# One scan instruction over two channel blocks in a selective state-space kernel

## Chip, core and metric

The kernel runs on one core of a Trainium2 chip. The metric is the device time of one execution, in microseconds (us). Before the change the median is 7764.41 us.

## What is computed

Two Mamba layers over 8192 steps and 1024 channels with 16 states each, with normalisation around them, and then a soft mixture of experts. The change is in the recurrence of the Mamba layers, which stands in the reference as:

```
dA = jnp.exp(jnp.einsum('bld,dn->bldn', delta, A))
dBu = jnp.einsum('bld,bln,bld->bldn', delta, Bm, u)
def step(h, inp):
    dA_t, dBu_t, C_t = inp
    h = dA_t * h + dBu_t
    return (h, jnp.einsum('bdn,bn->bd', h, C_t))
```

Before it come an input projection, a causal convolution of 4 taps with SiLU, the projections that give delta, B and C, and a softplus. After it come the skip u*D, the gate silu(z) and the output projection.

## The kernel before

**Tiling.** The sequence is cut into 16 chunks of T = 512 steps. Both layers give 32 chunks, numbered G. The 1024 channels are 8 blocks of 128 (the partitions). A chunk has 128 *slots*: k, b = divmod(slot, 4). Of k (0 to 31), k // 16 is the half (which 4 blocks) and k % 16 the state n; b is the block in the half. Two neighbouring slots are a *pair*, 0 to 63, and a chunk has 64.

**Per slot.** ScalarE (ACT) writes decay = exp(delta * -A) into a PSUM ring of 4 tiles (L855). GpSimd (POOL) writes bu = w * B for the two blocks of a pair in one instruction of 1024 elements (L1082) into a ring of 3 pairs. VectorE (DVE) scans a slot, h = decay * h + bu over 512 steps (L1162). The scan's first state is h_last of the chunk before, which ACT saves once per k, so 32 times per chunk (L888). TensorE (PE) then turns the four blocks of state k into PSUM, 128 steps at a time (tile ("state", k, j), L591), and acc += C * turned follows: three of four such tiles go to DVE as SCALAR_TENSOR_TENSOR (L1182), the fourth to ACT as a product (L871), which POOL sums (L1097, L1106). For even k it is tile j = 0 that goes to ACT, for odd k it is j = 3.

**The turn ring.** All turned tiles of a chunk (128 states, 8 "skip" tiles of u*D, L599, which ACT copies into acc at L878, and 8 "y" tiles, L607, which DVE gates at L1191) use two PSUM banks in turn. PE fills a bank only when the tile before the last one has been taken. A state tile of group k stands one slot after its group: tile (k, j) at slot 4k + 5 + j. ACT takes its tiles two slots after the slot where they stand. The first STT of a half into acc waits for ACT's copy of that skip tile.

**The order.** Every engine runs an order written out beforehand, slot by slot. At each slot DVE has its scan, then the turned tiles of that slot. PE has the turned tiles of the slot, then matmuls of the projections of this and the next chunk, which a timetable spreads. ACT has the decay, then products and copies, then what it takes from the projections. Four times a chunk it applies SiLU to four blocks (L760 and L798), with a table load ahead and one behind, at slots 43 and 65 (u), 116, and slot 1 of the next chunk (z). POOL has, per pair, the sums and products of delta at the pairs of W_AT, then bu, then the sums of SUM_AT.

The waits that the change touches are:

```
act.wait_ge(scanned, G * SLOTS_BODY + (s + 1 - DEC_RING + C_SCAN))        # decay_of
pool.wait_ge(scanned, G * SLOTS_BODY + (s + 2 - 2 * BU_RING + C_SCAN))    # inputs
dve.wait_ge(decay_set, G * SLOTS_BODY + (s + 1))                          # scan
dve.wait_ge(bu_set, G * PAIRS + (s // 2 + 1 + C_BU))
```

## Time and profile before

| | before |
|---|---|
| median of 3 runs | 7764.41 us (7763.73 to 7766.31) |
| span of the profiled execution | 7761.4 us |
| DVE busy | 7373.2 us, 95% |
| PE busy | 7045.9 us, 91% |
| POOL busy | 6604.5 us, 85% |
| ACT busy | 5872.5 us, 76% |

The 32 chunks fill the time from about 90 us to about 7190 us; the mixture of experts is the rest. The profiled execution is one run of its own. Instructions of an engine overlap at their ends, so what one costs in a queue is the distance of two starts, and that is less than its duration.

### The profile page before, as it was taken

How to read it: one execution, taken by the hardware profiler on the slowest of the kernel's cores; microseconds unless marked ns; L12 is line 12 of the kernel's file. 1: busy time of each engine (PE TensorE's matmuls, PEld its weight loads, DVE VectorE, ACT ScalarE, POOL GpSimd, SP SyncE). 2: the span in 40 equal slices, each digit the busy share in tenths (PEclk: the TensorE clock that was granted, in tenths of full speed). 3: DMA queues.
4: the chain of work that ended last, by engine and by line, in shares of the span. 5: the costliest groups of instructions: out<-in, count | busy, mean ns of one | idle time of the engine just before them, and what ended most of it. 6: DMA issues, size and time to landing. Idle time of an engine off the chain costs nothing. (4 is left out here: it accounts for less than half of the span.)

```text
span 7761.4 us, 100822 instructions
## 1 busy us (share of the span) xinstructions
PE 7045.9 (91%) x31116; PEld 4002.2 (52%) x31116; DVE 7373.2 (95%) x8275; ACT 5872.5 (76%) x11175; POOL 6604.5 (85%) x2871
## 2 busy tenths in 40 slices
PE   7899999999999999999999999999999999987799
PEld 3555555555555555554555555545555555554664
DVE  6999999999999999999999999999999999999655
ACT  7787788887877888777777777777777777775564
POOL 5999999999999999999999999999999999998010
PEclk9999999999999999999999999999999999998899
DMA  2221121112221211122211111111111111111665
GB/s 91 60 66 66 61 66 59 55 62 66 66 66 61 66 59 55 62 68 66 66 50 56 48 52 54 55 55 56 49 55 50 51 54 55 55 50 41 246 232 184
DMA packets 230984, 549.66 MB, mean 71 GB/s; under 512 B 27120, under 2 KB 27376, under 8 KB 210864
## 3 DMA queue, kind: packets, MB, share of 16 engines
q1 hardware_dynamic: 201776, 491.81, 19.9%
q10 hardware_dynamic: 28672, 51.39, 1.8%
q8 instruction: 252, 4.13, 0.2%
q14 instruction: 284, 2.33, 0.1%
HBM read 441.39 MB, written 101.71 MB: 70 GB/s over the span
## 5 line engine op out<-in xcount | busy, mean ns | idle before, releaser
L1082 POOL TENSOR_TENSOR bu<-w,b_rep 128x1024 f32<-128x1024 f32 x2048 | 4806.9, 2365 | 541.8 <-DVE h L1162 532.5
L1162 DVE TENSOR_TENSOR_SCAN h<-decay,h_last,bu 128x512 f32<-128x512 f32 x3840 | 4813.9, 1274 | 13.9 <-ACT decay L855 13.9
L591 PEld LDWEIGHTS turn<-ident_m,h 128*128 128x128 f32 x16384 | 1952.1, 142 | 2702.7 <-DVE acc L1182 1315.3
L855 ACT ACTIVATE decay<-delta,neg_a 128x512 f32<-128x512 f32 x4096 | 2777.4, 690 | 647.6 <-DVE h L1162 609.5
L591 PE MATMUL turn<-ident_m,h 128*128 128x128 f32 x16384 | 2558.2, 280 | 421.0 <-DVE acc L1182 348.2
L1182 DVE SCALAR_TENSOR_TENSOR acc<-turn,c_now,acc 128x512 f32<-128x512 f32 x3072 | 2243.7, 730 | 72.1 <-ACT c_now L883 43.1
L871 ACT ACTIVATE prod<-turn,c_now 128x512 f32<-128x512 f32 x1024 | 701.0, 685 | 504.2 <-PE turn L591 369.0
L1097 POOL TENSOR_TENSOR prod<-prod 128x1024 f32<-128x1024 f32 x448 | 1057.6, 2361 | 10.6 <-ACT prod L871 10.6
L513 PE MATMUL proj<-x_conv,w_in 128*128 128x512 f32 x2048 | 1046.3, 603 | 4.5 <-ACT x_conv L845 1.3
L513 PE MATMUL proj<-x_gate,w_in 128*128 128x512 f32 x2048 | 1019.8, 595 | 0.0
L513 PE MATMUL proj<-conv_in,conv_diag 128*128 128x512 f32 x1984 | 996.6, 594 | 0.0
L513 PE MATMUL proj<-zy,w_out 128*128 128x512 f32 x1024 | 505.6, 596 | 23.0 <-ACT u L756 20.5
L513 PE MATMUL proj<-w_out,zy 128*128 128x512 f32 x1024 | 504.4, 599 | 0.9 <-DVE zy L1191 0.9
L513 PEld LDWEIGHTS proj<-x_conv,w_in 128*128 128x128 f32 x2048 | 328.3, 193 | 123.5 <-issue 91.7
L513 PEld LDWEIGHTS proj<-x_gate,w_in 128*128 128x128 f32 x2048 | 324.1, 191 | 98.0 <-issue 91.8
L1162 DVE TENSOR_TENSOR_SCAN h<-decay,zeros_m,bu 128x512 f32<-128x512 f32 x256 | 320.1, 1272 | 46.7 <-POOL bu L1082 43.6
L513 PEld LDWEIGHTS proj<-conv_in,conv_diag 128*128 128x128 f32 x1984 | 313.8, 191 | 90.7 <-issue 89.1
L1064 POOL TENSOR_TENSOR delta<-delta,w 128x1024 f32<-128x1024 f32 x128 | 302.4, 2362 | 40.7 <-ACT w L789 40.7
L599 PE MATMUL turn<-d_diag,u 128*128 128x128 f32 x2048 | 288.6, 285 | 48.5 <-DVE acc L1182 44.2
L738 ACT ACTIVATE conv_diag<-ident_m,par 128x128 f32<-128x128 f32 x992 | 316.5, 394 | 0.4
L1071 POOL TENSOR_TENSOR w<-delta,u 128x1024 f32<-128x1024 f32 x128 | 302.5, 2363 | 0.3
L599 PEld LDWEIGHTS turn<-d_diag,u 128*128 128x128 f32 x2048 | 252.9, 194 | 74.3 <-DVE acc L1182 60.1
(161 smaller groups left out, 5690.6 us busy)
## 6 DMA issues: line engine op xcount, KB each, us to landing
b_rep<-b_rows SPq DMA_DIRECT2D x1024, 256.0 KB, 3.3
x_gate<-xt SPq DMA_DIRECT2D x32, 1024.0 KB, 7.0
xt<-stage ACTq DMA_DIRECT2D x128, 256.0 KB, 2.4
x_conv<-xt SPq DMA_DIRECT2D x31, 1024.0 KB, 6.9
x_gate<-in_x_dram SPq DMA_DIRECT2D x16, 1024.0 KB, 6.7
x_l<-in_x_dram SPq DMA_DIRECT2D x16, 1024.0 KB, 9.5
m_l<-xt SPq DMA_DIRECT2D x16, 1024.0 KB, 7.8
x<-x_l SPq DMA_DIRECT2D x16, 1024.0 KB, 6.3
```

What stands on the lines that cost most here:

```text
L513: mm = pe.matmul(out[0:lhs.shape[1], :], lhs, rhs, start=n == 0, stop=n == count - 1)
L591: mm = pe.transpose(out[:, b * P:(b + 1) * P], h[:, (G * GROUPS + k) % H_RING, b, j * P:(j + 1) * P], ident[:])
L599: mm = pe.matmul(out[:, b * P:(b + 1) * P], u[:, hf * HB + b, j * P:(j + 1) * P], d_diag[:, hf * HB + b, :], start=True, stop=True)
L738: act.activation(conv_diag[:, b % 2, k, :], ident[:], ACT.Copy, scale=par[:, STATES + k, b:b + 1])
L855: act.activation(decay[:, (G * SLOTS_BODY + s) % DEC_RING, :], delta[:, blk, :], ACT.Exp, scale=neg_a[:, n, blk:blk + 1]).then_inc(decay_s ...
L871: act.activation(prod[:, V_BUFFER[q], k % 2, :], turn[:, BANK[tile], :], ACT.Copy, scale=c_now[:, j, n:n + 1]).then_inc(v_done, 1)
L1064: pool.tensor_tensor(delta[:, lo:lo + 2, :], delta[:, lo:lo + 2, :], w[:, lo:lo + 2, :], ALU.add).then_inc(delta_set, 1)
L1071: pool.tensor_tensor(w[:, lo:lo + 2, :], delta[:, lo:lo + 2, :], u[:, lo:lo + 2, :], ALU.mult).then_inc(w_set, 2)
L1082: pool.tensor_tensor(bu[:, (G * PAIRS + s // 2) % BU_RING, :, :], w[:, blk:blk + 2, :], b_rep[:, g % B_RING, :].unsqueeze(1).to_broadcast( ...
L1097: pool.tensor_tensor(total, total, prod[:, V_BUFFER[q]], ALU.add).then_inc(vsum_set, 1)
L1162: dve.tensor_tensor_scan(h[:, (G * GROUPS + k) % H_RING, b, :], decay[:, (G * SLOTS_BODY + s) % DEC_RING, :], bu[:, (G * PAIRS + s // 2) % ...
L1182: dve.scalar_tensor_tensor(out, src, scalar, out, ALU.mult, ALU.add).then_inc(x_done, 1)
```

## The change

The scan now runs once per pair, over 1024 elements. The two blocks stand one behind the other, so at element 0 of each the decay is set to zero once at the start (DVE writes column 0 of the decay ring; ACT writes columns 1 to 511 only), and bu's column 0 holds the block's first state instead of the product (POOL writes columns 1 to 511). With a zero decay the state there becomes exactly that value. The first states of a half chunk (16 states x 4 blocks) are worked out ahead: POOL multiplies A and delta at step 0 ("exponent"), ACT takes the exponential, POOL forms w * B at step 0, multiplies the exponential by h_last and adds ("state"). ACT copies two columns per pair into bu (head). B at step 0 goes through DRAM: ACT stores 16 values, SP loads them to all partitions. Three entries of W_AT move to earlier pairs. DVE's order within a pair becomes: scan, then all turned tiles of both slots. ACT's becomes: head, both decays, then everything else of both slots.

```diff
-W_AT = {13: ('sum', 2), 19: ('product', 2), 25: ('sum', 3), 27: ('product', 3), 47: ('sum_next', 0), 51:
-        ('product_next', 0), 56: ('sum_next', 1), 63: ('product_next', 1)}
+W_AT = {13: ('sum', 2), 19: ('product', 2), 25: ('sum', 3), 27: ('product', 3), 47: ('sum_next', 0), 50:
+        ('product_next', 0), 53: ('sum_next', 1), 57: ('product_next', 1)}
+HEAD_AT = {26: ('exponent', 1), 30: ('state', 1), 54: ('exponent_next', 0), 62: ('state_next', 0)}
+HEAD_EXP_AT = {57: ('exp', 1), 115: ('exp_next', 0)}
+BFIRST_AT = 24
...
+        def load_first(X):
+            sp.wait_ge(bfirst_stored, X * 16 + 16)
+            if X > 0:
+                sp.wait_ge(hfirst_set, 2 * X)
+            sp.dma_start(b_first[:], d["b_row_first"][X].partition_broadcast(P)).then_inc(bfirst_in, 16)
...
+                if k == BFIRST_AT and not kind.last:
+                    load_first(G + 1)
...
-            act.activation(decay[:, (G * SLOTS_BODY + s) % DEC_RING, :], delta[:, blk, :], ACT.Exp,
+            act.activation(decay[:, (G * SLOTS_BODY + s) % DEC_RING, 1:T], delta[:, blk, 1:T], ACT.Exp,
...
+        def head(G, p):
+            k, pr = divmod(p, 2)
+            hf, n = divmod(k, STATES)
+            if p % (PAIRS // 2) == 0:
+                act.wait_ge(hfirst_set, 2 * G + hf + 1)
+            act.wait_ge(scanned, G * SLOTS_BODY + (2 * (p - BU_RING) + 2 + C_SCAN))
+            act.copy(bu[:, (G * PAIRS + p) % BU_RING, :, 0], h_first[:, hf, n, 2 * pr:2 * pr + 2]).then_inc(head_set, 1)
...
-                    decay_of(G, kind, k, b)
+                    if b % 2 == 0:
+                        head(G, s // 2)
+                        decay_of(G, kind, k, b)
+                        decay_of(G, kind, k, b + 1)
...
-            pool.tensor_tensor(bu[:, (G * PAIRS + s // 2) % BU_RING, :, :], w[:, blk:blk + 2, :],
-                               b_rep[:, g % B_RING, :].unsqueeze(1).to_broadcast([P, 2, T]), ALU.mult).then_inc(bu_set, 1)
+            pool.tensor_tensor(bu[:, (G * PAIRS + s // 2) % BU_RING, :, 1:T], w[:, blk:blk + 2, 1:T],
+                               b_rep[:, g % B_RING, 1:T].unsqueeze(1).to_broadcast([P, 2, T - 1]), ALU.mult).then_inc(bu_set, 1)
+        def first_exponent(X, hf):
...
+            pool.tensor_tensor(a_first[:], neg_a[:, :, blks], delta[:, blks, 0].unsqueeze(1).to_broadcast([P, STATES, HB]),
+                               ALU.mult).then_inc(exponent_set, 1)
+        def first_state(X, hf):
...
+            pool.tensor_tensor(h_first[:, hf], w[:, blks, 0].unsqueeze(1).to_broadcast([P, STATES, HB]),
+                               b_first[:].unsqueeze(2).to_broadcast([P, STATES, HB]), ALU.mult).then_inc(hfirst_set if fresh else first_step, 1)
...
+        dve.memset(decay[:, :, 0:1], 0.0).then_inc(heads_zero, 1)
+        def scan(G, kind, p):
+            k, pr = divmod(p, 2)
+            dve.wait_ge(decay_set, G * SLOTS_BODY + (2 * p + 2))
+            dve.wait_ge(bu_set, G * PAIRS + (p + 1 + C_BU))
+            dve.wait_ge(head_set, G * PAIRS + (p + 1))
...
+            dve.tensor_tensor_scan(h[:, (G * GROUPS + k) % H_RING, 2 * pr:2 * pr + 2, :].rearrange("p b t -> p (b t)"),
+                                   decay[:, at:at + 2, :].rearrange("p b t -> p (b t)"),
+                                   bu[:, (G * PAIRS + p) % BU_RING, :, :].rearrange("p b t -> p (b t)"), 0.0,
+                                   ALU.mult, ALU.add).then_inc(scanned, 2)
...
-                scan(G, kind, k, j)
+                if s % 2 == 0:
+                    scan(G, kind, s // 2)
```

**What moves on DVE.** First the order of DVE around slots 34 to 39 of a chunk. The rows that write h are scans, those that write acc take turned tiles. Before:

```order
L1162 SCALAR_TENSOR_TENSOR h<-decay,h_last,bu 128x512
L1182 SCALAR_TENSOR_TENSOR acc<-turn,c_now,acc 128x512
L1162 SCALAR_TENSOR_TENSOR h<-decay,h_last,bu 128x512 x3
L1182 SCALAR_TENSOR_TENSOR acc<-turn,c_now,acc 128x512
L1162 SCALAR_TENSOR_TENSOR h<-decay,h_last,bu 128x512
```

After, in the same place:

```order
L1255 SCALAR_TENSOR_TENSOR h<-decay,bu 128x1024
L1277 SCALAR_TENSOR_TENSOR acc<-turn,c_now,acc 128x512 x2
L1255 SCALAR_TENSOR_TENSOR h<-decay,bu 128x1024 x2
L1277 SCALAR_TENSOR_TENSOR acc<-turn,c_now,acc 128x512 x2
L1255 SCALAR_TENSOR_TENSOR h<-decay,bu 128x1024
```

Two takings that had a scan between them now stand next to each other. Where a gated y tile falls into a pair, three stand in a row. After, at slots 118 and 119:

```order
L1255 SCALAR_TENSOR_TENSOR h<-decay,bu 128x1024
L1277 SCALAR_TENSOR_TENSOR acc<-turn,c_now,acc 128x512
L1286 TENSOR_TENSOR zy<-turn,zy 128x512
L1277 SCALAR_TENSOR_TENSOR acc<-turn,c_now,acc 128x512
```

Before, a scan stood between the second and the third of these.

**What moves on ACT.** Now ACT's order from slot 8 to slot 10 of a chunk; the rows that write acc are copies of skip tiles. Before:

```order
L888 COPY h_last<-h 128x4
L855 ACTIVATE decay<-delta,neg_a 128x512
L878 COPY acc<-turn 128x512
L738 ACTIVATE conv_diag<-ident_m,par 128x128 x4
L855 ACTIVATE decay<-delta,neg_a 128x512
L878 COPY acc<-turn 128x512
```

After:

```order
L935 COPY h_last<-h 128x4
L925 COPY acc<-turn 128x512
L767 ACTIVATE conv_diag<-ident_m,par 128x128 x4
L898 COPY bu<-h_first 128x2
L888 ACTIVATE decay<-delta,neg_a 128x511 x2
L925 COPY acc<-turn 128x512
```

Between the two copies one decay and the head are added.

## Rows read from the trace of the kernel before

**Rows 1.** The page, busy time of each engine over the span.

```profile
PE 7045.9 (91%) x31116; PEld 4002.2 (52%) x31116; DVE 7373.2 (95%) x8275; ACT 5872.5 (76%) x11175; POOL 6604.5 (85%) x2871
```

**Rows 2.** One 500 us stretch inside the chunks: busy time by engine, clock, DMA.

```profile
3000.00:3500.00 500.00, 461.92 (x2066) 260.28 (x2065) 494.38 (x527) 394.55 (x751) 461.47 (x200) 0.99 0.19 61
```

**Rows 3.** Groups, 2000 to 6000 us: busy, mean ns | idle before, releasers.

```profile
L1162 DVE TENSOR_TENSOR_SCAN h<-decay,h_last,bu 128x512 f32<-128x512 f32 x2186 | 2740.4, 1274 | 8.2 <-ACT decay L855 8.2
L1082 POOL TENSOR_TENSOR bu<-w,b_rep 128x1024 f32<-128x1024 f32 x1158 | 2717.4, 2364 | 302.8 <-DVE h L1162 297.0 <-DMA b_rep<-b_rows 5.0
L855 ACT ACTIVATE decay<-delta,neg_a 128x512 f32<-128x512 f32 x2314 | 1568.5, 690 | 359.8 <-DVE h L1162 342.1 <-ACT stage L804 7.3 <-ACT conv_in L845 5.9
...
L1182 DVE SCALAR_TENSOR_TENSOR acc<-turn,c_now,acc 128x512 f32<-128x512 f32 x1734 | 1266.5, 730 | 37.4 <-ACT c_now L883 25.2 <-PE turn L591 12.0
...
L888 ACT COPY h_last<-h 128x4 f32<-128x4 f32 x578 | 108.4, 188 | 0.0
```

**Rows 4.** All waits of DVE, 2000 to 6000 us: total us, times, longest.

```profile
DVE acc L1182 <- ACT c_now L883: 25.2, 18, 1.4
DVE acc L1182 <- PE turn L591: 12.0, 23, 2.0
DVE h L1162 <- ACT decay L855: 10.5, 19, 1.9
```

**Rows 5.** Timeline of DVE, slots 4 to 8: start, length, instruction [idle before].

```profile
3423.87 3.64 DVE L1162 TENSOR_TENSOR_SCAN h<-decay,h_last,bu 128x512 f32<-128x512 f32 x3
3427.95 0.75 DVE L1182 SCALAR_TENSOR_TENSOR acc<-turn,c_now,acc 128x512 f32<-128x512 f32 x1 [0.44 <-PE turn L591]
3428.62 1.27 DVE L1162 TENSOR_TENSOR_SCAN h<-decay,h_last,bu 128x512 f32<-128x512 f32 x1
3429.81 0.73 DVE L1182 SCALAR_TENSOR_TENSOR acc<-turn,c_now,acc 128x512 f32<-128x512 f32 x1
3430.45 1.27 DVE L1162 TENSOR_TENSOR_SCAN h<-decay,h_last,bu 128x512 f32<-128x512 f32 x1
3433.13 0.75 DVE L1182 SCALAR_TENSOR_TENSOR acc<-turn,c_now,acc 128x512 f32<-128x512 f32 x1 [1.40 <-ACT c_now L883]
```

**Rows 6.** Timeline of ACT in the same place.

```profile
3430.14 0.59 ACT L878 COPY acc<-turn 128x512 f32<-128x512 f32 x1 [0.85 <-PE turn L599]
3430.63 1.28 ACT L738 ACTIVATE conv_diag<-ident_m,par 128x128 f32<-128x128 f32 x4
3431.81 0.68 ACT L855 ACTIVATE decay<-delta,neg_a 128x512 f32<-128x512 f32 x1
3432.42 0.58 ACT L878 COPY acc<-turn 128x512 f32<-128x512 f32 x1
```

**Rows 7.** Timeline of PE: a skip tile, and a turn that waited for DVE.

```profile
3429.05 1.06 PE L599 MATMUL turn<-d_diag,u 128*128 128x128 f32 x8
...
3433.94 0.66 PE L591 MATMUL turn<-ident_m,h 128*128 128x128 f32 x4 [0.93 <-DVE acc L1182]
```

**Rows 8.** Groups of DVE behind the chunks: one operation at two widths.

```profile
L1418 DVE TENSOR_TENSOR run_top<-run_top,logits 128x1024 f32<-128x1024 f32 x16 | 19.2, 1199 | 10.7 <-ACT logits L1454 10.7
...
L1637 DVE TENSOR_TENSOR top_d<-run_top 128x512 f32<-128x512 f32 x1 | 0.7, 693 | 0.3 <-PEq L1961 0.3
```

**Rows 9.** Timeline of ACT around one SiLU, at slot 65.

```profile
3526.11 1.28 ACT L760 ACT_TABLE_LOAD   x1
3527.40 1.91 ACT L760 ACTIVATE u<-u 128x2048 f32<-128x2048 f32 x1
3529.33 1.28 ACT L703 ACT_TABLE_LOAD   x1
3530.63 1.91 ACT L855 ACTIVATE decay<-delta,neg_a 128x512 f32<-128x512 f32 x3
```

**Rows 10.** Timeline of POOL: three bu back to back.

```profile
3408.52 6.98 POOL L1082 TENSOR_TENSOR bu<-w,b_rep 128x1024 f32<-128x1024 f32 x3
```

**Rows 11.** A small POOL operation, 2000 to 6000 us.

```profile
L1055 POOL TENSOR_TENSOR nmr_x<-neg_mean,rstd_x 128x4 f32<-128x4 f32 x5 | 1.0, 206 | 0.0
```

65 lines of the change are left out of this document (55 added, 10 removed).

## The prediction

> **What bounds the kernel now.** I read the page first: DVE is busy for 95% of the span, PE for 91%, POOL for 85% [rows 1]. Then one stretch inside the chunks: DVE 494 of 500 us, PE 462, POOL 461, ACT 395 [rows 2]. So DVE is the bound, with three engines close behind. Last I read who keeps DVE waiting. From 2000 to 6000 us there are 578 saves of h_last at 32 per chunk [rows 3], so 18.06 chunks, 221.5 us each. All waits of DVE there are 25.2 + 12.0 + 10.5 = 47.7 us [rows 4], which is 2.6 us per chunk. The other 218.9 us are DVE's instructions one behind the other. The 18 waits of 1.4 us, one per chunk, all have one place: the taking at slot 8, which needs ACT's copy of a skip tile.
>
> **What the change takes away.** One scan of two. A scan lasts 1.274 us, but costs a queue the distance of two starts: three in a row take 3.64 us, so (3.64 - 1.27) / 2 = 1.18 [rows 5]. What is its fixed part? An STT of the same width lasts 0.730, a scan 0.544 more [rows 3]. A TENSOR_TENSOR of 1024 elements lasts 1.199 against 0.693 for 512: 0.506 for 512 elements [rows 8]. I take 0.535 for a pass over 512 elements, between these two, and two passes for a scan, 1.07. What is left of 1.18 is 0.11 us, and 0.115 with 1.19 for a scan that an STT follows (3428.62 to 3429.81 [rows 5]). A pair's scan then costs 2.25 us in the queue instead of 2.37. Per chunk that is 64 x 0.115 = 7.4 us, or 236 us for 32 chunks. The bounds are nothing (a pair's scan costs two scans) and 2 x 0.693 - 1.199 = 0.19 us per pair [rows 8], 12 us per chunk.
>
> The Trainium skill, "VectorE: DVE Perf Modes", section on the TRN2 errata, says that the fixed latency is paid once per instruction, so that one large tile pays once what many small tiles pay each, and gives (N + 151) / 0.96 ns for an fp32 tensor_tensor. Its fixed 157 ns would make the gain 2048 x 0.157 = 322 us, by that page an estimate. The rows here agree on the duration (0.693 for 512) but show that neighbours overlap, so I keep 0.115.
>
> **What it adds, and what hides it.**
> - ACT: 64 head copies per chunk. A copy of 4 columns lasts 0.188 [rows 3]. ACT goes from 0.79 of a chunk [rows 2] to at most 0.84 with 64 x 0.188 = 12 us, so on average it is covered; ends of instructions overlap, and I take 0.08 each. If not covered, see below.
> - POOL: 8 small operations per chunk, each at least 0.2 [rows 11]; I take 0.3, so 2.4 us. POOL has 64 + 24 large ones at (6.98 - 2.36) / 2 = 2.31 [rows 10], 203 us. So POOL needs about 206 us per chunk against DVE's 211.5 + stalls. Adding up POOL's operations from pair 42 to pair 57, where seven extra ones now lie, gives 46.5 us against DVE's 46 and a lead of one ring: within 0.1 to 0.5. I book 0.3 us.
> - SP and the store of B's first column: one small transfer each per chunk, issued at k = 24, while ACT's store is at slot 76 (k = 19) and the consumer at pair 62. Nothing waits. Before the first chunk it is a transfer in series, about 3 us once.
>
> **The stalls that the new order makes.** Here I disagree with the plain gain. Times below are from the DVE instruction named.
> 1. *Two takings of the same bank with no scan between.* PE refills a bank only once it is taken. An STT lasts 0.73, PE starts 0.06 after it (3433.88 to 3433.94) and takes 0.66 [rows 5, 7], and the next STT starts some 0.04 behind: 1.49 us from start to start. Where an ACT tile lies between two DVE tiles (pairs 4 and 19), DVE is ready after 0.64 and loses 0.85. Where three DVE tiles stand in a row (pairs 11, 12, 13, 59, 60, 61) it is ready after 1.26 and loses 0.23. Sum: 1.7 + 1.4 = 3.1 us per chunk. Before, a scan of 1.19 covered each.
> 2. *Slot 8, the wait of 1.4 us.* Let T be the start of the STT at slot 6. PE's skip tile starts at T + 0.79 and takes 1.06, ACT's copy ends its part at T + 2.4, the four conv_diag take 1.18, then head 0.08, two decays 1.24, the copy 0.6, and DVE goes on at T + 5.6. (Before: 3427.95 to 3433.13, 5.18, with one decay of 0.61 less and PE 0.3 later [rows 5, 6].) DVE is ready at T + 2 x 0.64 + 2.25 = T + 3.53. The wait is 2.05 instead of 1.4.
> 3. *SiLU.* From the first table load to the next decay ACT is away for 3530.63 - 3526.11 = 4.52 us [rows 9]. Before, the next decay was due three scans and four or five takings after the ring let ACT go; now both decays of a pair are due together. From the end of scan p - 2: head and decays 1.36, SiLU 4.52, head and decays 1.45, so 7.35, against 2 x 2.25 + n x 0.64 for the n takings of three pairs. At slot 1, n is 4: 7.07, so a loss of 0.3 to 0.4. At slot 65, n is 4 too, and ACT arrives late in chunks with a norm: 0.3 to 0.8, I take 0.5. At slot 43 n is 6 and the 0.85 of pair 19 comes on top: none. At slot 116: none.
> 4. ACT's own lag in the crowded first half (skip copies at pairs 17, 18, norms): 0.4.
>
> Stalls after: 3.1 + 2.05 + 0.9 + 0.4 + 0.3 = 6.8 us per chunk, 4.2 more than the 2.6 of now.
>
> **The sum.** 7.4 - 4.2 = 3.2 us per chunk, 32 chunks: 102 us, less 3 us at the start: 99 us. The profiled span is 7761.4, 3.0 below the median of the runs, so the median goes from 7764.4 to about 7665, which is 1.3% faster. PE's work per chunk does not change, and its idle time in a chunk is about 17 us [rows 2].
>
> **The rivals.**
> - *A. The gain comes through.* The stalls overlap with each other, as one gives the next its slack. For it: now only 2.6 us of 221.5 are lost, with engines as full. Against it: items 1 and 2 lie in DVE's own chain, and no slack elsewhere helps them. Time: 7764.4 - 236 + 3 = 7531. Chance 0.22. The page above would give still more.
> - *B. POOL becomes the bound (slower).* Its bu rows now have 511 elements and start one element late. No row shows such a shape. POOL has 24 x 2.31 + 2.4 = 57.8 us of other work, so it equals the present chunk of 221.5 when a bu costs (221.5 - 57.8) / 64 = 2.56 us, 11% above 2.31. From there on the kernel is slower; at 2.65 the chunk is 227.4, + 189 us: 7953. For it: POOL is full to 93% as it is, so little is enough. Against: bu and the sums, of different patterns, last the same, 2.36. Chance 0.08.
> - *C. The stalls are larger than I book,* about 10 to 11.5 us: ACT, with decays that are due in twos, falls behind all through the first half. 7764 +- 35. Chance 0.14.
> - *D. The change doesn't shorten the scan:* a scan over two PSUM banks costs 2.37. Then only the stalls are left, 4.2 x 32 = 134: 7900. Against: the two passes per element of rows 3 and 8. Chance 0.06.
>
> **How the numbers follow.** My forecast has 0.50, with its own range of 7600 to 7740 (stalls 4.5 to 9 us per chunk). The range for all takes in A and most of C: 7535 to 7790; below lies the upper bound of the fixed part, above lie B and D. A measurement of this kernel tells 0.2%, 15 us, from no change. Faster: 0.50 + 0.22 + a bit of C = 0.75. Same: 0.07, from C. Slower: B, D and the rest of C, 0.18.
>
> **What would show it.** The group of scans: 128x1024, mean 2.34 us (rival D: 2.5). The waits of DVE: "acc <- c_now" of about 2.05 once per chunk where 1.4 was; "acc <- PE turn" of 0.85 twice and of about 0.2 six times per chunk; "h <- decay" about 0.9 per chunk; "h <- bu" nearly none. bu on POOL at 2.36 (rival B: above 2.6). Head copies at 0.2. If DVE's waits sum to 2.6 per chunk, A is right; if they sum to over 10, C. I would be wrong also if the three waits of a scan cost time of their own in DVE's queue, or if PE, not asked for here, is late at the second tile of most pairs.

## The result and the profile after

The changed kernel takes 7890.7 us (median of 4 runs, 7889.7 to 7891.9) against 7764.1 before. The ratio is 1.0162, with a 95% interval from 1.0148 to 1.0177: 1.6% slower, where 1.3% faster was forecast, and 101 us above the upper end of the range.

The page of the changed kernel, busy time of each engine over its span of 7889.6 us (before: [rows 1]):

```profile
PE 7014.4 (89%) x31116; PEld 4070.2 (52%) x31116; DVE 7096.4 (90%) x6228; ACT 6063.2 (77%) x13283; POOL 6671.7 (85%) x3115
```

DVE has 277 us less to do than in [rows 1], and yet the kernel takes 127 us more. So the scans got cheaper, and the gain went into waiting. The groups from 2000 to 6000 us show the same, with the columns of [rows 3]:

```profile
L1138 POOL TENSOR_TENSOR bu<-w,b_rep 128x1022 f32<-128x1022 f32 x1136 | 2669.2, 2366 | 327.3 <-DVE h L1255 327.2
L1255 DVE TENSOR_TENSOR_SCAN h<-decay,bu 128x1024 f32<-128x1024 f32 x1136 | 2567.3, 2276 | 94.5 <-ACT decay L888 79.2 <-issue 7.8 <-POOL bu L1138 4.8
L888 ACT ACTIVATE decay<-delta,neg_a 128x511 f32<-128x511 f32 x2272 | 1479.8, 686 | 312.0 <-DVE h L1255 311.6
...
L1277 DVE SCALAR_TENSOR_TENSOR acc<-turn,c_now,acc 128x512 f32<-128x512 f32 x1703 | 1199.0, 734 | 172.9 <-PE turn L620 139.9 <-ACT c_now L930 31.1
...
L898 ACT COPY bu<-h_first 128x2 f32<-128x2 f32 x1136 | 216.1, 190 | 20.2 <-ACT stage L837 14.3 <-DVE h L1255 2.7 <-ACT conv_in L878 2.5
```

The scan lasts 2.276 us where two of 1.274 stood. The shape of 511 elements costs POOL nothing (2.366 against 2.364), and a head copy costs 0.19. What has changed is the last part of the two DVE rows, the idle time before them. All waits of DVE in the same 4000 us, against 25.2 + 12.0 + 10.5 us in [rows 4]:

```profile
DVE acc L1277 <- PE turn L620: 139.9, 230, 1.9
DVE h L1255 <- ACT decay L888: 79.2, 84, 2.5
DVE acc L1277 <- ACT c_now L930: 31.1, 18, 1.7
DVE h L1255 <- issue: 7.8, 18, 0.5
DVE h L1255 <- POOL bu L1138: 4.8, 18, 0.3
DVE h L1255 <- ACT h_last L935: 2.7, 2, 1.3
```

**Figures per chunk.** From here on I use three numbers per chunk, worked out from each trace over the chunks 9 to 26 (of 0 to 31): the *period*, the mean distance between the first scans of two chunks; the *idle* time of DVE, the sum of all gaps over 30 ns before its scans and takings; and DVE's *own work*, the difference of the two. Before they are 221.4, 2.65 and 218.8 us. After they are 225.4, 15.33 and 210.1. Own work fell by 8.7 and idle time rose by 12.7, where the forecast had 7.4 and 4.2. The difference of 4.0, times 32 chunks, is 128 us, and the runs differ by 127.

Two limits of these figures. The median less 32 periods is not the same for all kernels below: 677 to 678 us for the kernel before and the changed one, 682 to 694 us for the others. So periods and medians can disagree by up to half a us per chunk, and where a price is that small I give both. And own work is not durations alone: each wait also breaks the overlap of two neighbours on DVE, and the lost overlap is counted as own work.

By pair, the idle time of DVE is (us per chunk; pairs under 0.3 in both left out):

```
pair    before  after   before it stands, after
1        0.10   0.66    scan <- decay
3        0.53   0.35    taking <- turn
4        1.40   2.48    taking <- c_now 1.73, second taking <- turn 0.75
16        -     0.35    second taking <- turn
19        -     1.82    scan <- decay 1.07, second taking <- turn 0.75
22       0.48   1.03    scan <- decay 0.88, scan <- h_last 0.15
28        -     0.32    scan <- decay
31       0.13   0.37    taking <- turn
33        -     1.57    scan <- decay
35        -     1.10    taking <- turn
55        -     1.34    second taking <- turn
59        -     2.35    taking <- turn 1.87, scan <- issue 0.43
```

### The profile page after: what moved, and what is told of

It reads as the page before. It is cut to its first block and busy times, and to the rows that moved or that the text cites. A ratio compares the mean times of both kernels' runs of the same rounds, so it can differ in the third digit from the quotient of the medians.

```text
span 7889.6 us, 101470 instructions
## 1 busy us (share of the span) xinstructions
PE 7014.4 (89%) x31116; PEld 4070.2 (52%) x31116; DVE 7096.4 (90%) x6228; ACT 6063.2 (77%) x13283; POOL 6671.7 (85%) x3115
## 3 DMA queue, kind: packets, MB, share of 16 engines
q14 instruction: 289, 2.37, 0.1%
## 5 line engine op out<-in xcount | busy, mean ns | idle before, releaser
L1138 POOL TENSOR_TENSOR bu<-w,b_rep 128x1022 f32<-128x1022 f32 x2048 | 4810.2, 2365 | 593.1 <-DVE h L1255 593.0
L1255 DVE TENSOR_TENSOR_SCAN h<-decay,bu 128x1024 f32<-128x1024 f32 x2048 | 4628.4, 2276 | 210.5 <-ACT decay L888 138.5
L620 PEld LDWEIGHTS turn<-ident_m,h 128*128 128x128 f32 x16384 | 1997.7, 143 | 2744.9 <-issue 1409.7
L888 ACT ACTIVATE decay<-delta,neg_a 128x511 f32<-128x511 f32 x4096 | 2667.8, 686 | 566.7 <-DVE h L1255 565.3
L1277 DVE SCALAR_TENSOR_TENSOR acc<-turn,c_now,acc 128x512 f32<-128x512 f32 x3072 | 2163.9, 734 | 313.2 <-PE turn L620 255.4
L542 PE MATMUL proj<-x_gate,w_in 128*128 128x512 f32 x2048 | 1040.4, 605 | 37.6 <-ACT zy L827 37.6
L898 ACT COPY bu<-h_first 128x2 f32<-128x2 f32 x2048 | 389.7, 190 | 43.8 <-ACT stage L837 25.5
```

Of the source, the lines that this page charges most:

```text
L542: mm = pe.matmul(out[0:lhs.shape[1], :], lhs, rhs, start=n == 0, stop=n == count - 1)
L620: mm = pe.transpose(out[:, b * P:(b + 1) * P], h[:, (G * GROUPS + k) % H_RING, b, j * P:(j + 1) * P], ident[:])
L888: act.activation(decay[:, (G * SLOTS_BODY + s) % DEC_RING, 1:T], delta[:, blk, 1:T], ACT.Exp, scale=neg_a[:, n, blk:blk + 1]).then_inc(dec ...
L898: act.copy(bu[:, (G * PAIRS + p) % BU_RING, :, 0], h_first[:, hf, n, 2 * pr:2 * pr + 2]).then_inc(head_set, 1)
L1138: pool.tensor_tensor(bu[:, (G * PAIRS + s // 2) % BU_RING, :, 1:T], w[:, blk:blk + 2, 1:T], b_rep[:, g % B_RING, 1:T].unsqueeze(1).to_broa ...
L1255: dve.tensor_tensor_scan(h[:, (G * GROUPS + k) % H_RING, 2 * pr:2 * pr + 2, :].rearrange("p b t -> p (b t)"), decay[:, at:at + 2, :].rearr ...
```

## What happens at two of these places

**Pair 59, behind the SiLU of slot 116.** ACT in the changed kernel (start, length, instruction, idle before):

```profile
3904.51 0.18 ACT L935 COPY h_last<-h 128x4 f32<-128x4 f32 x1
3904.71 1.28 ACT L831 ACT_TABLE_LOAD   x1
3906.01 1.92 ACT L831 ACTIVATE zy<-zy 128x2048 f32<-128x2048 f32 x1
3907.94 1.28 ACT L732 ACT_TABLE_LOAD   x1
3909.24 0.19 ACT L898 COPY bu<-h_first 128x2 f32<-128x2 f32 x1
3909.34 1.29 ACT L888 ACTIVATE decay<-delta,neg_a 128x511 f32<-128x511 f32 x2
3910.57 0.67 ACT L918 ACTIVATE prod<-turn,c_now 128x512 f32<-128x512 f32 x1
```

PE in the same place:

```profile
3908.12 1.02 PE L542 MATMUL proj<-x_gate,w_in 128*128 128x512 f32 x2
3911.29 0.66 PE L620 MATMUL turn<-ident_m,h 128*128 128x128 f32 x4 [2.14 <-ACT prod L918]
3911.78 1.10 PE L542 MATMUL proj<-x_gate,w_in 128*128 128x512 f32 x2
3912.68 1.06 PE L620 MATMUL turn<-ident_m,h 128*128 128x128 f32 x4
3913.53 1.06 PE L636 MATMUL turn<-ident_m,acc 128*128 128x128 f32 x4
3914.39 1.83 PE L542 MATMUL proj<-x_gate,w_in 128*128 128x512 f32 x2
3916.05 0.60 PE L620 MATMUL turn<-ident_m,h 128*128 128x128 f32 x4
```

And DVE:

```profile
3910.72 2.29 DVE L1255 TENSOR_TENSOR_SCAN h<-decay,bu 128x1024 f32<-128x1024 f32 x1 [0.42 <-issue]
3913.78 0.75 DVE L1277 SCALAR_TENSOR_TENSOR acc<-turn,c_now,acc 128x512 f32<-128x512 f32 x1 [0.77 <-PE turn L620]
3914.63 0.69 DVE L1286 TENSOR_TENSOR zy<-turn,zy 128x512 f32<-128x512 f32 x1
3916.70 0.75 DVE L1277 SCALAR_TENSOR_TENSOR acc<-turn,c_now,acc 128x512 f32<-128x512 f32 x1 [1.38 <-PE turn L620]
```

ACT is away for 4.5 us. Its decays then wait for nothing, but its product stands behind head and decays, and ends at 3911.24. Until then ACT holds one of the two banks, and PE, which works in order, stands for 2.14 us with its projections behind the turn. What follows is dearer than the wait: PE's four transposes take 1.06 us instead of 0.60. The windows show why (us, then busy time of PE, PEld, DVE, ACT and POOL, granted clock, DMA share, GB/s):

```profile
3905.00:3911.00 6.00, 4.15 (x19) 2.16 (x17) 5.58 (x6) 5.96 (x7) 6.00 (x4) 1.00 0.40 87
3911.00:3913.00 2.00, 1.71 (x8) 1.15 (x9) 2.00 (x1) 1.73 (x5) 2.00 (x2) 0.90 0.93 306
3913.00:3915.00 2.00, 2.00 (x9) 1.72 (x8) 1.13 (x3) 2.00 (x6) 2.00 (x1) 0.50 1.06 451
3915.00:3917.00 2.00, 2.00 (x8) 0.93 (x7) 0.62 (x2) 0.36 (x1) 1.92 (x5) 0.75 0.81 331
```

The granted clock is 0.50 for 3.4 us, which is 1.2 instead of 2.4 GHz, beginning 1.3 us after PE's idle time. DVE has little to scan just here (it gates a y tile and takes), so both of PE's late tiles show: 0.77 and 1.38 us.

How much of this is the clock can be read from the same trace. In all 18 chunks PE stands idle here for 2.14 or 2.15 us, but in 4 of them the clock stays at 1.00. One of the four, DVE:

```profile
3235.53 0.75 DVE L1277 SCALAR_TENSOR_TENSOR acc<-turn,c_now,acc 128x512 f32<-128x512 f32 x1 [0.28 <-PE turn L620]
...
3237.27 0.75 DVE L1277 SCALAR_TENSOR_TENSOR acc<-turn,c_now,acc 128x512 f32<-128x512 f32 x1 [0.39 <-PE turn L620]
```

Without the fall DVE's takings at pair 59 wait 0.66 us in each of the four, with it 2.24 to 2.34 us in each of the 14 others. The heavy DMA traffic of the stretch shown is not the reason: in chunks 11, 17, 22 and 25, which have a fall here too, DMA's share is at most 0.12 there and the takings wait 2.27 to 2.34 us. So a fall costs DVE 1.6 us here, and PE's idle time without one 0.66. Pair 35 is alike: 0.70 us in the 13 chunks without a fall at pair 33, 2.02 to 2.23 us in the 5 with one. Together the falls at these two places make 1.7 of the 15.3 us of idle time per chunk in this one profiled execution.

**Pair 55, a moved sum on POOL.** POOL in the changed kernel, then ACT:

```profile
3889.77 4.70 POOL L1138 TENSOR_TENSOR bu<-w,b_rep 128x1022 f32<-128x1022 f32 x2
3894.39 2.38 POOL L1180 TENSOR_TENSOR prod<-prod 128x1024 f32<-128x1024 f32 x1
3896.70 2.38 POOL L1138 TENSOR_TENSOR bu<-w,b_rep 128x1022 f32<-128x1022 f32 x1
```

```profile
3893.42 0.69 ACT L918 ACTIVATE prod<-turn,c_now 128x512 f32<-128x512 f32 x1
3896.87 0.69 ACT L918 ACTIVATE prod<-turn,c_now 128x512 f32<-128x512 f32 x1 [2.76 <-PE turn L620]
```

The product of 3896.87 starts 0.1 us after POOL's sum over earlier products ends (3894.39 + 2.38 = 3896.77). The view names the turn as its releaser, but the turn it reads was done at 3895.5 (0.60 us from 3894.94), so it is the sum that frees the product's buffer. ACT then gives its bank back late, and DVE's second taking waits 1.34 us (3898.34 to 3899.68). POOL is late there, since its steps on delta stand at pairs 50, 53 and 57 instead of 51, 56 and 63, with an exponent at 54. That was a reading; the kernels *no_heads_w* and *w_late2* below test it.

## The experiments

Each was timed beside the kernel before, whose median stayed between 7763.7 and 7765.3 us. The first group walks from the kernel before to the changed one, the last splits the gain.

| kernel | median us | ratio to before (95%) | period | idle | own work |
|---|---|---|---|---|---|
| before | 7764.1 | 1 | 221.4 | 2.65 | 218.8 |
| order_act | 7819.7 | 1.0071 (1.0056 to 1.0086) | 223.1 | 4.21 | 218.9 |
| order_dve | 7900.9 | 1.0176 (1.0161 to 1.0191) | 225.5 | 5.39 | 220.1 |
| order_both | 7904.7 | 1.0181 (1.0166 to 1.0196) | 225.6 | 5.74 | 219.9 |
| pair_sync | 7969.0 | 1.0262 (1.0247 to 1.0277) | 227.6 | 7.33 | 220.2 |
| no_heads_w | 7762.1 | 0.9996 (0.9986 to 1.0006) | 220.8 | 10.88 | 209.9 |
| no_heads | 7797.6 | 1.0042 (1.0028 to 1.0056) | 222.4 | 12.34 | 210.0 |
| copies_only | 7822.8 | 1.0073 (1.0058 to 1.0088) | 222.8 | 12.71 | 210.1 |
| after | 7890.7 | 1.0162 (1.0148 to 1.0177) | 225.4 | 15.33 | 210.1 |
| w_late2 | 7835.6 | 1.0093 (1.0076 to 1.0110) | 223.6 | 13.55 | 210.0 |
| after_no_tables | 7752.0 | 0.9984 (0.9975 to 0.9994) | 220.8 | 10.92 | 209.9 |
| before_no_tables | 7748.3 | 0.9978 (0.9969 to 0.9988) | 220.8 | 2.14 | 218.7 |
| skip_early | 7911.3 | 1.0187 (1.0170 to 1.0204) | 225.6 | 15.38 | 210.2 |
| lag2 | 7939.3 | 1.0224 (1.0209 to 1.0239) | 226.5 | 16.49 | 210.0 |
| act_fine | 7992.5 | 1.0293 (1.0277 to 1.0308) | 228.1 | 17.27 | 210.8 |
| mixed | 7737.9 | 0.9965 (0.9952 to 0.9978) | 220.4 | 10.04 | 210.3 |
| mixed_w | 7700.8 | 0.9917 (0.9902 to 0.9932) | 219.1 | 8.80 | 210.3 |
| const_start | 7595.6 | 0.9783 (0.9769 to 0.9798) | 215.8 | 4.16 | 211.6 |
| twos_const | 7798.3 | 1.0044 (1.0027 to 1.0061) | 222.2 | 9.47 | 212.7 |
| single_all | 7675.4 | 0.9887 (0.9872 to 0.9901) | 218.2 | 6.41 | 211.8 |

### The coarse order alone: order_both, order_dve, order_act

The kernel before, with single scans of 512, in the order of the changed kernel on both engines, on DVE alone and on ACT alone:

```diff
 # DVE (order_both, order_dve)
-                scan(G, kind, k, j)
+                if s % 2 == 0:
+                    scan(G, kind, *divmod(s, J))
+                    scan(G, kind, *divmod(s + 1, J))
                 for tile in TURN_AT[s]:
 # ACT (order_both, order_act)
-                    decay_of(G, kind, k, b)
+                    if b % 2 == 0:
+                        decay_of(G, kind, k, b)
+                        decay_of(G, kind, k, b + 1)
```

> The kernel before, single scans of 512 and no first states worked out, but in the coarse order of the change: on DVE both scans of a pair and then the turned tiles of both slots, on ACT both decays of a pair and then the rest of both slots. Theory 1 (the coarse order makes the stalls): the 15.3 us of stalls per chunk seen after the change appear here too, without the gain of the merged scan: about 12 us per chunk more than before, 8150 us, at least 8000. Theory 2 (the stalls come from the work that was added on ACT and POOL, heads and first states): close to before, under 7850.

> The kernel before with DVE's coarse order alone: two scans, then the tiles of both slots; ACT as before. Theory 1: the waits of DVE's takings (PE turn and the copy at slot 8) rise as after the change, from 2.1 to 6 to 8 us per chunk, about 7900 to 7950 us, and scans wait little for decays. Theory 2: no change, 7764.

> The kernel before with ACT's coarse order alone: both decays of a pair first; DVE as before. Theory 1: scans wait for decays around the SiLUs, 2 to 3 us per chunk more, 7830 to 7860 us. Theory 2: no change, 7764.

The order alone costs 4.2 us per chunk, almost all of it on DVE (4.1 alone; ACT's alone 1.7; the two don't add). The waits of order_both, 2000 to 6000 us:

```profile
DVE acc L1184 <- PE turn L591: 60.1, 161, 0.8
DVE acc L1184 <- ACT c_now L883: 31.5, 18, 1.8
DVE h L1164 <- ACT decay L855: 7.1, 24, 2.0
```

By pair these stand where item 1 and item 2 of the prediction put them: 0.75 at pairs 4 and 19, 0.09 to 0.31 at pairs 11 to 13 and 59 to 61, and 1.75 for the skip tile. Missed were 0.35 at pair 5, 0.36 at 35 and 0.18 at 16. The idle time is 5.7 us, the forecast for the new order was 6.8. So this part of the argument holds. Own work rises by 1.1 besides: the durations of DVE's instructions sum to 0.9 less, but neighbours overlap by 17.9 instead of 19.9 us per chunk. The total of 7905 us lies between the two theories (at least 8000, under 7850). In order_act the scans hardly wait (0.09 us per chunk for decays), against what was expected: the 1.6 us more of idle time stand at the takings of pairs 4, 23 and 59.

### Giving and taking in twos: pair_sync

order_both, in which a scan waits for both decays of its pair and gives both ring places back at once, as a merged scan must:

```diff
-            dve.wait_ge(decay_set, G * SLOTS_BODY + (s + 1))
+            dve.wait_ge(decay_set, G * SLOTS_BODY + (s // 2 * 2 + 2))
...
-                                   ALU.mult, ALU.add).then_inc(scanned, 1)
+            if b % 2 == 1:
+                ins.then_inc(scanned, 2)
```

> The coarse order of both engines with single scans of 512, as in order_both, but each pair's first scan waits for both decays, and the ring places are given back once per pair: the waits of a merged scan without its speed. Order_both has 225.6 us per chunk, 5.7 of them stalls. Theory A (a merged scan stalls because it takes and gives back its inputs in twos): stalls rise to 9 us per chunk and more, 8000 us or more. Theory B (the faster DVE meets bursts of ACT, POOL and PE that it did not outrun before): as order_both, 7905, plus at most 20 us.

It costs 1.9 us per chunk more. The wait for decays goes from 0.39 to 1.83 us per chunk, at pairs 19 (0.21 to 0.82), 22 (to 0.50) and 33 (0.07 to 0.34), where the changed kernel has it too. With 7.3 us of idle time and 7969 us it too lies between its two theories (9 us and 8000, or 7925 at most).

### The merged scan without heads: no_heads_w and no_heads

The changed kernel without all that the first states need: POOL writes bu's 512 columns again and the second block of a pair goes on from column 0 with a decay of zero, so no state is carried from chunk to chunk. no_heads_w also has the old W_AT:

```diff
-                        head(G, s // 2)
-            dve.wait_ge(head_set, G * PAIRS + (p + 1))
-                    if s in HEAD_EXP_AT:
+                    if False:
-                if p in HEAD_AT:
+                if False:
 # no_heads_w besides
-W_AT = {13: ('sum', 2), 19: ('product', 2), 25: ('sum', 3), 27: ('product', 3), 47: ('sum_next', 0), 50:
-        ('product_next', 0), 53: ('sum_next', 1), 57: ('product_next', 1)}
+W_AT = {13: ('sum', 2), 19: ('product', 2), 25: ('sum', 3), 27: ('product', 3), 47: ('sum_next', 0), 51:
+        ('product_next', 0), 56: ('sum_next', 1), 63: ('product_next', 1)}
```

> No_heads (7798) with the products and sums of delta at their old pairs (51, 56 and 63 for 50, 53 and 57). What is left against pair_sync is then the merged scan alone. If the moved POOL work makes the waits at pairs 55 and 59 (1.1 and 1.5 us per chunk): 7720 to 7770, faster by 1 to 2.5 us per chunk. If those waits come from the SiLU and the turn ring: 7798 +- 15.

> The changed kernel without the first states: no head copies on ACT, no exponents and states on POOL, no load of B's first column, and POOL forms bu over all 512 columns, so each block starts from its own bu and not from the chunk before. Coarse order and merged scan stay. Theory 1: ACT has some 5 us per chunk less, which eases the SiLU places a little: 7830 to 7880. Theory 2: the stalls go, about 7530 to 7600.

From pair_sync to no_heads_w own work falls by 10.3 us per chunk (220.2 to 209.9), while idle time rises by 3.6: a DVE that is done earlier finds ACT and PE not ready. (2.2 us of it stand before scans under "issue", with no releaser in the profile, but at pairs 19 and 33, where the other kernels wait for decays.) What is left in the period is 6.7 us per chunk, about what order and twos had cost (4.2 + 1.9): the kernel stands where it stood before. (What the 10.3 consist of, twos_const tells below.) The moved sums alone then cost 1.5 us per chunk (no_heads against no_heads_w), which is pair 55's 1.10 and 0.9 more at pair 59, less 0.65 at pair 56. The heads make the last 3.1. By the medians the two are 1.1 and 2.9. For no_heads itself neither range came true: its 7798 us lie between 7600 and 7830.

### Which part of the heads: copies_only

The changed kernel with ACT's 64 head copies from a tile of zeros, without POOL's exponents, products and states, without ACT's exponentials of them and the transfer of B's first column. Every block starts from zero in every chunk.

```diff
-            if p % (PAIRS // 2) == 0:
-                act.wait_ge(hfirst_set, 2 * G + hf + 1)
-                    if s in HEAD_EXP_AT:
+                    if False:
-                if p in HEAD_AT:
+                if False:
```

> The changed kernel with ScalarE's 64 copies of a block's first state per chunk, taken from a tile of zeros, and without everything that works the first states out: GpSimd's exponents, products and states, ScalarE's exponentials of them, the loads and the store of B's first column. Each block of channels then starts from a zero state in every chunk, so the work left out is the carry from chunk to chunk. The heads as a whole cost 3.1 us a chunk (225.4 against 222.4 without them). If ScalarE's copies make that (64 of 0.19 us are 12 us a chunk, on the engine whose lateness the scan waits for), 225 us a chunk and about 7880. If GpSimd's small steps and the waits for them make it, 222.6 and about 7800.

The first theory falls: 64 copies of 0.19 us cost 0.4 us per chunk by the periods, 0.8 by the medians (7822.8 against 7797.6), of 3.1 and 2.9 for the heads. POOL's eight small steps and ACT's two exponentials, some 3 us of work per chunk, cost 2.7: 0.8 at pair 59, 0.6 at 33, 0.4 at 35 and 0.3 each at 28 and 55. The trace of the changed kernel has them dearer than I had booked, from 2000 to 6000 us:

```profile
L1157 POOL TENSOR_TENSOR h_first<-w,b_first 128x64 f32<-128x64 f32 x36 | 12.6, 351 | 0.0
L1147 POOL TENSOR_TENSOR a_first<-neg_a,delta 128x64 f32<-128x64 f32 x33 | 12.1, 366 | 0.0
L1163 POOL TENSOR_TENSOR a_first<-a_first,h_last 128x64 f32<-128x64 f32 x34 | 11.6, 341 | 0.0
L1166 POOL TENSOR_TENSOR h_first<-h_first,a_first 128x64 f32<-128x64 f32 x34 | 10.9, 320 | 2.7
```

Of the 2.7 us, the 0.8 at pair 59 and the 0.4 at pair 35 are PE's clock: in copies_only it falls at pair 59 in 5 of the 18 chunks and never at pair 33, in the changed kernel in 14 and in 5. Without a fall pair 59 has 1.10 us of idle time here and 1.09 there. For the rest, whether it is POOL's time or ACT's exponentials between decays, this kernel does not tell apart.

### The moved sums in the full change: w_late2

The changed kernel with four of POOL's steps later (product_next 0 at 51 instead of 50, the rest as below):

```diff
-        ('product_next', 0), 53: ('sum_next', 1), 57: ('product_next', 1)}
+        ('product_next', 0), 56: ('sum_next', 1), 61: ('product_next', 1)}
-HEAD_AT = {26: ('exponent', 1), 30: ('state', 1), 54: ('exponent_next', 0), 62: ('state_next', 0)}
+HEAD_AT = {26: ('exponent', 1), 30: ('state', 1), 56: ('exponent_next', 0), 62: ('state_next', 0)}
```

> The changed kernel, with four of GpSimd's small steps later in the chunk: product_next 0 at pair 51 instead of 50, sum_next 1 at 56 instead of 53, product_next 1 at 61 instead of 57, exponent_next at 56 instead of 54. Nothing else differs. The theory that the sums moved to earlier pairs are what pairs 55 and 59 wait for (1.34 and 2.35 us a chunk in the changed kernel; without the heads the same move cost 1.5 us a chunk) expects 1 to 2 us a chunk back, 223.4 to 224.4 us a chunk and about 7835 to 7860 us. The rival, that these waits come from ScalarE's own lateness and only show at GpSimd's sums, expects 7890 within 15 us.

It gives back 1.9 us per chunk and 55 us in all. Pair 55's wait is gone, pair 59's falls from 2.35 to 0.66, and 0.97 comes at pair 56, where the scan now waits mostly for bu (0.64). The largest waits:

```profile
DVE acc L1277 <- PE turn L620: 105.4, 236, 1.4
DVE h L1255 <- ACT decay L888: 82.5, 89, 2.5
DVE acc L1277 <- ACT c_now L930: 30.9, 18, 1.7
DVE h L1255 <- POOL bu L1138: 11.2, 12, 1.2
```

So the reading of pair 55 is shown, and pair 59 is where two causes meet. With the steps later PE's idle time there is 1.68 us in place of 2.14, and its clock does not fall there in any of the 18 chunks; 0.66 is also what the takings of the changed kernel wait in the chunks without a fall.

### SiLU without its table loads: after_no_tables, before_no_tables

Both kernels with Identity instead of Silu and no load of tables behind it. The activations stay at 1.91 us, ACT is away some 2 instead of 4.5 us, and the output lacks the SiLU.

```diff
-            ... u[:, hf * HB:hf * HB + HB, :], ACT.Silu).then_inc(u_set, 1)
-            exp_tables()
+            ... u[:, hf * HB:hf * HB + HB, :], ACT.Identity).then_inc(u_set, 1)
```

> The changed kernel with Identity in place of SiLU in the layers and without the two table loads around each (u and the gate are not passed through SiLU): ACT is away for 1.9 us instead of 4.5, four times a chunk. If the stalls that grew with the faster DVE hang on ACT's absence (pairs 1, 22, 33, 59 and what follows on PE): 5 us per chunk less and more, 7740 or less. If the engines are too full everywhere: 7850 or more.

> The same edit in the kernel before (Identity for SiLU, no table loads), as the control. Its waits for decays are 0.6 us per chunk: 7740 to 7760. If the change is then faster than before, ACT's absences are what turned its sign.

Before, the loads cost 0.6 us per chunk: the fine order hides them. After, they cost 4.6 of period and 4.4 of idle time. Pair 59's wait falls from 2.35 to 0.15, pair 33's from 1.57 to nothing, pair 1's from 0.66 to 0.22, pair 35's from 1.10 to 0.70; the 1.03 us of pair 22 come at pair 28 instead. Pair 55's 1.34 stays (1.32), as POOL makes it. Against its own control the change is then level, 7752.0 to 7748.3 us: with SiLU's table loads gone 123 of the 127 us between the two kernels are gone, but it does not become faster, which was the sign set for "what turned its sign", and the 7740 us expected was missed by 12.

### Three attempts to take single waits away: skip_early, lag2, act_fine

skip_early has the skip tile of slot 8 at slot 3 (and one of slot 38 at 37), lag2 has ACT take its turned tiles later, act_fine has ACT do each decay in its own slot again:

```diff
 # skip_early
-SKIP_AT = ((7, 4, 5, 8), (31, 33, 35, 38))
+SKIP_AT = ((7, 4, 5, 3), (31, 33, 35, 37))
 # lag2
-SUM_LAG = 1
+SUM_LAG = 2
 # act_fine
-                        decay_of(G, kind, k, b)
-                        decay_of(G, kind, k, b + 1)
+                    decay_of(G, kind, k, b)
```

> The changed kernel with two skip tiles moved: (0, 3) from slot 8 to 3, (1, 3) from slot 38 to 37. This takes away the wait for the copy at slot 8 (1.7 us per chunk) and the two places where an ACT tile lies between two DVE tiles (0.75 each): up to 3.2 us per chunk. If these waits stand in DVE's own chain and nothing else is late there: 7790 us. If the other engines are late anyway and the stalls move on: 7860 or more.

> The changed kernel with every turned state tile one slot later (SUM_LAG 2 for 1). A pair then holds tiles j = 0, 1 or 2, 3 of one state, so DVE takes one or two per pair where it took none or two, and ACT one or none where it took none or two. If the bunching within pairs feeds the stalls: 7700 to 7800 us. If ACT's total load and heads make them: 7890 +- 20.

> The changed kernel with ACT's second decay behind the rest of the first slot, as the order stood before; heads, merged scan and DVE's order stay. If ACT's coarse order takes part in the stalls (order_act alone cost 55 us): 7840 to 7870 us. If only the merged scan's need for both decays counts: 7890, or slower, as the second decay comes later.

None pays, and of the three only skip_early and act_fine came out as one of the theories had it; lag2's 7939 us lie above both. In skip_early pair 4's 2.48 us are gone, and pair 3 has 2.97 instead of 0.35: the work of ACT and PE in pairs 1 to 4 is the limit, not the place of one copy. In lag2 the waits for turns fall by 1.2 us per chunk, but those for decays rise from 4.54 to 5.66, those for bu from 0.26 to 1.25, and the skip tile's from 1.73 to 2.09. In act_fine the second decay of a pair stands behind a slot's products and copies, and the scan, which needs both, waits 7.2 us per chunk for decays. So ACT's coarse order, dear on its own, is still better for a merged scan than the fine one.

### Both kinds of scan in one kernel: mixed and mixed_w

The changed kernel, in which the pairs with waits run as two single scans in the old fine order on DVE and ACT, with the heads as before. mixed_w adds pair 28 and w_late2's four places:

```diff
+SINGLE = (0, 1, 3, 4, 5, 11, 12, 13, 16, 19, 21, 22, 31, 32, 33, 34, 35, 57, 58, 59, 60, 61)
+        def scan_one(G, s):
+            k, b = divmod(s, HB)
+            dve.wait_ge(decay_set, G * SLOTS_BODY + (s + 1))
+            dve.tensor_tensor_scan(h[:, (G * GROUPS + k) % H_RING, b, :], decay[:, (G * SLOTS_BODY + s) % DEC_RING, :],
+                                   bu[:, (G * PAIRS + s // 2) % BU_RING, b % 2, :], 0.0, ALU.mult, ALU.add).then_inc(scanned, 1)
...
                 if s % 2 == 0:
                     scan(G, kind, s // 2)
+                elif s // 2 in SINGLE:
+                    scan_one(G, s)
```

> The changed kernel, but at 22 of the 64 pairs (0, 1, 3, 4, 5, 11 to 13, 16, 19, 21, 22, 31 to 35, 57 to 61: where stalls stood) two single scans in the old order of DVE and ACT, with the same heads. 42 merged pairs keep 42 x 0.155 = 6.5 us per chunk. If the stalls belong to the coarse places: they fall to 5 or less, 7680 to 7740. If they move to the next place where an engine is short: 7800 or more.

> The mixed kernel (merged scans for most pairs, two single scans in the old fine order at the pairs where the scan or the product waited), with pair 28 single too and GpSimd's four small steps at the later pairs of w_late2. If the sums at pairs 50 to 57 are what pair 55 waits for (1.3 us a chunk), and the merged scan is worth 0.17 us for each of 41 pairs, 219.0 to 219.5 us a chunk and 7690 to 7710 us, clearly below the kernel before. If the waits come from ScalarE's total work, it stays at 220.4 us a chunk, 7738 within 15 us.

mixed beats the kernel before by 26 us, mixed_w by 63. The time of mixed is in its expected range, but its reason is not: idle time was to fall to 5 us or less and is 10.0. The last step, from mixed, gives 37 us (1.3 us per chunk). In mixed_w idle time is 8.8 us instead of 15.3. Own work is 210.3 us, as low as with merged scans everywhere, though 23 of the 64 pairs have two scans. That was not expected, and one row has the clue: in mixed_w a single scan lasts 1.209 us.

```profile
L1248 DVE TENSOR_TENSOR_SCAN h<-decay,bu 128x512 f32<-128x512 f32 x830 | 997.4, 1209 | 39.2 <-ACT decay L889 38.9
```

In [rows 3] it lasts 1.274. What differs is its start value: a constant here, a column of h_last there.

### Start value or merging: const_start, twos_const, single_all

const_start is the kernel before with a constant start value, twos_const is pair_sync with it; both leave out the carry from chunk to chunk. single_all computes all of the reference: it is mixed_w with all 64 pairs as single scans, so it keeps the first states and the heads of the change and merges nothing.

```diff
 # const_start, twos_const
-            start = zeros[:, 0:1] if kind.first or kind.enters else h_last[:, s:s + 1]
+            start = 0.0
 # single_all
-SINGLE = (0, 1, 3, 4, 5, 11, 12, 13, 16, 19, 21, 22, 28, 31, 32, 33, 34, 35, 57, 58, 59, 60, 61)
+SINGLE = tuple(range(64))
```

> The kernel before, with single scans in its own fine order, whose start value is the constant 0.0 instead of a column of h_last or of a tile of zeros. It leaves out the carry from chunk to chunk. If the start value read from a tile costs 0.06 us a scan (the mixed kernels' single scans, which have a constant one, last 1.209 us against 1.274 and are 1.129 before the next instruction against 1.188), DVE's own work falls by 128 x 0.059 = 7.5 us a chunk to about 211.3, and the period, with one to three us more of waits since ACT, PE and POOL are no faster, to 213 to 216: 7500 to 7600 us. The rival, that the merging of two scans makes the whole gain and the shorter single scans of the mixed kernels come from something else, expects 7764 within 15 us.

> pair_sync (single scans, coarse order, given and taken in twos) with the start value 0.0. Against no_heads_w only the merging of the two scans is left (own work 209.9, period 220.8). By the start value's 0.06 us a scan, own work is 220.2 - 7.5 = 212.7, the merging itself is worth 2.8 us of the 10.3 a chunk (0.044 us a pair), and the period is 222 to 224 with 9 to 11 us of waits, 7800 to 7850 us. If merging makes the whole gain, own work stays at 220.2 and the time at 7969.

> mixed_w with all 64 pairs as two single scans in the old fine order: the changed kernel's first states worked out ahead and its head copies, but no merged scan at all. The whole reference is computed. If the constant start value makes most of the gain and the fine order hides the absences of ACT, own work is about 211.5 us a chunk and the waits 5 to 8, so 216.5 to 219.5 and 7620 to 7715 us, below mixed_w's 7700.8 or equal to it. If the merged scans of 41 pairs are what makes mixed_w fast, it goes to 225 us a chunk and above 7850.

The scans from 2000 to 6000 us, first const_start:

```profile
L1162 DVE TENSOR_TENSOR_SCAN h<-decay,bu 128x512 f32<-128x512 f32 x2372 | 2816.5, 1206 | 22.7 <-ACT decay L855 22.5
```

then twos_const:

```profile
L1164 DVE TENSOR_TENSOR_SCAN h<-decay,bu 128x512 f32<-128x512 f32 x2304 | 2657.2, 1202 | 51.6 <-ACT decay L855 48.9 <-POOL bu L1084 1.7
```

One line of code in the kernel before, no merging, and 168 us are gone (without the carry it is a test, not a usable kernel). A scan that reads its start value from a tile costs 0.06 us more than one with a constant: start to start it is 1.188 against 1.129 us before an STT, and 1.184 against 1.123 before another scan. For 128 scans that is 7.6 us per chunk, and own work falls by 7.2 (218.8 to 211.6).

twos_const against no_heads_w leaves only the merging (and decays of 511 instead of 512 columns, 683 against 684 ns): own work 212.7 against 209.9, which is 2.8 us per chunk or 0.044 per pair. So of the 10.3 us between pair_sync and no_heads_w 7.5 are the start value, and 2.8 the merging. In period the merging gives 1.4 (222.2 against 220.8), while the order and the twos that come with it cost 6.4 (222.2 against 215.8). By the medians these are 1.1 and 6.3.

single_all confirms it from the other side: 7675.4 us, 1.1% faster than before, 215 us faster than the changed kernel and 25 faster than mixed_w. Its own work is 1.8 us above that of w_late2, its idle time 7.1 below. Its waits, 2000 to 6000 us:

```profile
DVE h L1248 <- ACT decay L889: 39.6, 34, 2.4
DVE acc L1291 <- PE turn L621: 38.5, 57, 3.3
DVE acc L1291 <- ACT c_now L931: 29.1, 18, 1.6
DVE h L1248 <- POOL bu L1142: 7.7, 18, 0.7
```

## Why the prediction was wrong

**What bounds the kernel** was right: DVE, with three engines close behind. "Close behind" was then not used enough. The forecast needed the gain to exceed the new stalls; the gain came, and the stalls were 15.3 us per chunk where 6.8 were booked. Two of its steps failed, item 3 and POOL's 0.3.

**The gain** was put at 7.4 us per chunk; own work fell by 8.7, and by 10.3 with the coarse order on both sides. The number is near, but the mechanism was half wrong. The pass was sized well (2.276 - 1.206 = 1.07 for two passes over 512, as booked). The 0.11 us that remained was called the scan's fixed part, which merging saves once. In fact 0.06 of it is the reading of the start value, and the change drops that for both scans of a pair, the remaining one too: 0.12 per pair from the constant, and 0.044 (coarse order) to 0.064 (2 x 1.129 - 2.194) from merging. The Trainium skill, "VectorE: DVE Perf Modes", section on the TRN2 errata, gives an fp32 tensor_tensor (N + 151) / 0.96 ns, so by that page a fixed part of 157 ns is paid once per instruction, an estimate for a scan. The 0.16 us per pair of pair_sync to no_heads_w (10.3 / 64) lies near it by chance, since the larger part is the start value. What merging alone gives is 0.136 in duration (2 x 1.206 - 2.276), not far from the page, but only 0.044 to 0.064 from start to start. That the booked 7.4 came near the measured fall of own work is luck too.

**Items 1 and 2, the same-bank takings and slot 8,** were right: in order_both 2.5 us where 3.1 were booked (0.75 at pairs 4 and 19, and 0.95 at the six others), and in the changed kernel 1.73 instead of 2.05.

**Item 3, SiLU,** is the first step that failed: 0.9 us booked, 4.4 measured (idle time of after against after_no_tables, for the table loads alone; 1.7 of it are the falls at pairs 59 and 33). It asked only when the next scan gets its decays. It did not follow the ACT tile that stands behind these decays: that product holds one bank of two, PE works in order and stands, in 14 of 18 chunks its clock then falls to half, and DVE's takings are late, by 1.6 us more with the fall than without. "At slot 116: none" is just the place of pair 59 with its 2.35 us. And slot 65 (pair 33), booked at 0.5, has 1.57 at the scan and 0.4 of the 1.10 at pair 35, that 0.4 again by falls of the clock. Slot 43 (pair 22), where "none" stood as well, has 1.03 against 0.48 before. Item 4, ACT's lag, booked at 0.4, is 1.07 at pair 19 and 0.32 at pair 28; without the giving and taking in twos (order_both) pair 19 has 0.21.

**POOL's stall, "I book 0.3",** is the second, and no smaller. The sum of POOL's time from pair 42 to 57 was compared with DVE's, with the lead of one ring, and for bu it was right (0.26). But bu isn't all that waits for POOL: ACT's products wait for its sums, and the way from there through the ring to DVE was not looked at. The moved sums cost 1.5 (without heads) to 1.9 us per chunk (with them), the small steps with the exponentials 2.7. These prices and SiLU's overlap at pairs 33, 35 and 59, so they don't add up to the difference.

**Head copies** on ACT were rightly held to be mostly covered: 0.4 us per chunk, 0.8 by the medians. The 3 us at the start came as forecast: the first scan begins at 99.04 instead of 96.10 us.

**The rivals.** B (bu dearer at 511 elements) and D (a scan over two banks no shorter) are excluded by the rows, 2.366 and 2.276 us (2.194 from start to start, where D had 2.37). A would have needed the waits to hide one another. C, ACT falling behind with decays in twos, was the right kind: the wait for decays is 4.5 us per chunk. But its 10 to 11.5 us of stalls, put at 0.14, were still below the 15.3 that came. Its time was not worked out well either: by the forecast's own sum 11.5 us of stalls make about 7812 us, not 7799.

**The sum as it should have been**, in us per chunk, each from two runs: constant start value -5.7 (const_start), coarse order and twos +6.4 (twos_const), merging -1.4 (no_heads_w), moved sums +1.5 (no_heads), heads +3.1 (after). That is +3.9, the measured difference of 4.0 but for rounding. By the medians over 32 chunks the same five are -5.3, +6.3, -1.1, +1.1 and +2.9. The forecast had -7.4 for the first and third, +3.9 for the second, and +0.3 for the last two.

In the "what would show it" list the sum of the waits, over 10 us, points at C. The sign nearest to what happened is "if PE, not asked for here, is late at the second tile of most pairs": PE is late at 230 takings in 17.75 chunks, 13 per chunk, so not in most pairs, but with 7.9 us per chunk it is more than half of all idle time.
